# Expert 0's weights split by ACT and DVE in the gap between two stages, in place of POOL during attention

## What is computed

```python
x = x + attention(layernorm(x), ctx, ctx)     # 16 heads of 16, rope, window of 64 keys
x = x + experts(layernorm(x))

def experts(x):                               # E = 8 experts, hidden size 1024
    probs = softmax(x @ router_w.T)
    p, i = top_k(probs, 2); p = p / p.sum(-1)
    for e in range(8):
        mask = (i == e).any(-1)
        mean_w = (p * (i == e)).sum() / max(mask.sum(), 1)
        h = silu(x @ gate_w[e].T) * (x @ up_w[e].T)
        out += mask * (h @ down_w[e].T) * mean_w
```

## Time and profile before

| | |
|---|---|
| median of 3 runs | 505.71 us (504.89 to 505.95) |
| the profiled execution | 505.44 us, its span from first to last instruction 503.5 us |
| PE busy | 447.7 us (89%) |
| DVE busy | 308.0 us (61%) |
| ACT busy | 264.9 us (53%) |
| POOL busy | 139.0 us (28%) |
| the chain of work that ended last | PE 65%, DVE 14%, issue 6%, ACT 6%, POOL 4%, DMA 3% |
| mean granted clock of TensorE | 0.96 |

### The profile page before, as it was taken

How to read it: one execution, slowest core, us unless ns; L and a number is a source line. 1 busy time by engine, 2 the same in 40 slices (tenths; PEclk the granted TensorE clock), 3 DMA queues, 4 the chain that set the end, 5 groups by cost and what they waited for, 6 DMA issues and landing times.

```text
span 503.5 us, 8805 instructions
## 1 busy us (share of the span) xinstructions
PE 447.7 (89%) x2747; PEld 365.6 (73%) x2747; DVE 308.0 (61%) x721; ACT 264.9 (53%) x847; POOL 139.0 (28%) x130
## 2 busy tenths in 40 slices
PE   3999999898988999517999999999999999999980
PEld 2656565565655565316999999999999999999980
DVE  3566889898989867542754737646366463663320
ACT  1297867676766778203545545546365453544330
POOL 5201135262717163340005023040130401304013
PEclk9999999999999999755999999999999999999996
DMA  7075202020202025435464546645465453312003
GB/s 231 28 208 196 79 21 64 5 63 6 62 7 61 8 59 176 152 92 149 126 199 77 168 127 152 191 83 160 136 143 178 87 161 114 38 38 33 6 0 36
DMA packets 23597, 49.36 MB, mean 98 GB/s; under 512 B 5288, under 2 KB 15080, under 8 KB 23292
## 3 DMA queue, kind: packets, MB, share of 16 engines
q10 hardware_dynamic: 6302, 23.29, 15.1%
q1 hardware_dynamic: 11102, 18.51, 11.9%
q0 software_dynamic: 6144, 6.97, 8.4%
HBM read 38.51 MB, written 12.74 MB: 102 GB/s over the span
## 4 chain that ended last, share of the span: by engine, by line
PE 65%; DVE 14%; issue 6%; ACT 6%; POOL 4%; DMA 3%; ACTq 1%; DVEq 0%; SPq 0%; POOLq 0%
PE b_o L638 9%; PE b_small L638 9%; PE b_s L625 8%; PE b_s L626 8%; PE b_s L627 8%; PE b_s L424 3%; ACT probs L743 3%; PE b_pt L625 3%; PE b_pt L627 3%; PE b_pt L626 3%; DVE negmax L994 2%; PE b_proj L478 2%; DVE xn L860 2%; PE b_pv L447 2%; DMA rows_sb<-in_rownum 2%
## 5 line engine op out<-in xcount | busy, mean ns | idle before, releaser
L743 ACT ACTIVATE probs<-b_s,negmax 100x100 f32<-100x100 f32 x256 | 85.6, 360 | 33.2 <-DVE negmax L994 33.0
L1192 POOL DMA_INDIRECT out<-y_sb,idnow x32 | 48.7, 1523 | 181.5 <-ACT y_sb L789 174.2
L772 ACT CAST h_hi<-h_sb 128x448 fp32r<-128x448 f32 x64 | 36.3, 567 | 88.1 <-DVE h_sb L1080 88.1
L625 PE MATMUL b_s<-x_hi,w_hi 128*128 128x448 f32 x192 | 72.4, 377 | 0.7 <-DVE x_lo L1070 0.7
L626 PE MATMUL b_s<-x_lo,w_hi 128*128 128x448 f32 x192 | 71.6, 373 | 0.0
L627 PE MATMUL b_s<-x_hi,w_lo 128*128 128x448 f32 x192 | 71.5, 372 | 0.0
L1084 DVE TENSOR_TENSOR h_lo<-h_sb,h_hi 128x448 fp32r<-128x448 f32 x64 | 40.2, 628 | 40.5 <-ACT h_hi L772 40.5
L1089 DVE TENSOR_TENSOR w_lo<-w_raw,w_hi 128x1024 fp32r<-128x1024 f32 x42 | 51.5, 1225 | 13.6 <-ACT w_hi L777 13.6
L743 ACT ACTIVATION_READ_ACCUMULATOR probs<-b_s,negmax 100x1 f32 x256 | 56.7, 221 | 0.0
L424 PE MATMUL b_s<-kblk,qrot 128*100 128x400 f32 x128 | 54.3, 506 | 0.0
L1080 DVE TENSOR_TENSOR h_sb<-b_s,act 128x448 f32<-128x448 f32 x32 | 19.8, 620 | 45.1 <-PE b_s L627 45.1
(11 more groups left out here) (133 smaller groups left out, 964.2 us busy)
## 6 DMA issues: line engine op xcount, KB each, us to landing
w_raw<-in_ffw ACTq DMA_DIRECT2D x36, 512.0 KB, 3.9
xin<-slots SPq DMA_DIRECT2D x9, 449.8 KB, 4.5
slots<-in_padrows SPq DMA_DIRECT2D x8, 449.8 KB, 4.6
w_raw<-in_ffw ACTq DMA_DIRECT2D x1, 3072.0 KB, 10.1
w_raw<-in_ffw SPq DMA_DIRECT2D x6, 512.0 KB, 6.6
kblk<-krot SPq DMA_DIRECT2D x128, 12.5 KB, 1.8
out<-x_all SPq DMA_DIRECT2D x8, 200.0 KB
ctx_all<-in_ctxT SPq DMA_DIRECT2D x1, 1200.0 KB, 6.1
```

The lines of the kernel that those rows point to most:

```text
L625: pe.matmul(o, wh[:, c, cols], x_hi[:, c, :], start=(c == 0), stop=False)
L743: m = nc.scalar.activation(probs[:, N % 3, h, :], b_s[N % 3][0:S, h * S:(h + 1) * S], ACT.Exp, bias=negmax[:, N % 4, h:h + 1], accum_out=p ...
L772: nc.scalar.copy(h_hi[:, f, :], h_sb[:, f % 2, :]).then_inc(s_hhi, 1)
L1192: G.indirect_dma_start(out, bass.IndirectOffsetOnAxis(idnow[:, n:n + 1], 0), y_sb[:, n, :], None, bounds_check=TOK + TILE - 1, oob_is_err= ...
```

## The change

POOL no longer splits expert 0's weights. ACT issues their load in pair 1 as six chunks in place of one. After the last exponentials of attention, at `n == 0` of `i == 9`, ACT casts all six chunks, ahead of its copy `xn2T` of the last pair. DVE subtracts two chunks at the same place of its list, ahead of the last pair's `logits`, and the other four after `meanw`, ahead of the experts. SP no longer loads expert 1's weights; ACT issues these six loads after it has cast `x_hi` of the first tile, each when its chunk of `w_raw` has been subtracted. The counts that later waits look for are moved by one load accordingly.

```diff
@@ sync
-            sp.wait_ge(s_wlo, WCH)
-            for k in range(WCH):
-                sp.dma_start(w_raw[:, k * WC:(k + 1) * WC], ffw[1][:, k * WC:(k + 1) * WC]).then_inc(s_raw[k], 16)
             store_x2(NPAIR - 1)
@@ scalar
+            def weights_high(e, par, k):
+                a.wait_ge(s_raw[k], 16 * (e + 2))
+                cols = slice(k * WC, (k + 1) * WC)
+                nc.scalar.copy(w_hi[1 - par][:, cols], w_raw[:, cols]).then_inc(s_whi, 1)
+
                         nc.scalar.copy(probsT[:, M % 3].rearrange("p h s -> p (h s)"),
                                        b_pt[0:S, 0:QH * S]).then_inc(s_pTc, 1)
+                    if n == 0 and i == NPAIR + 1:
+                        for k in range(WCH):
+                            weights_high(-1, 1, k)
                     if n == 0 and 0 <= i - 2 < NPAIR:
                         x2_copy(i - 2)
                     if n == 1 and i == 1:
-                        a.dma_start(w_raw[:, :], ffw[0]).then_inc(s_raw0, 16)
+                        for k in range(WCH):
+                            a.dma_start(w_raw[:, k * WC:(k + 1) * WC],
+                                        ffw[0][:, k * WC:(k + 1) * WC]).then_inc(s_raw[k], 16)
...
             x_high(0)
+            for k in range(WCH):
+                reload(-1, k)
             for e in range(E - 1):
                 expert(e, e % 2, e + 2 < E)
@@ vector
+            def weights_low(e, par, k):
+                v.wait_ge(s_whi, WCH * (e + 1) + k + 1)
+                cols = slice(k * WC, (k + 1) * WC)
+                V.tensor_tensor(w_lo[1 - par][:, cols], w_raw[:, cols], w_hi[1 - par][:, cols],
+                                ALU.subtract).then_inc(s_wlo, 1)
...
+                    if n == 0 and i == NPAIR + 1:
+                        for k in range(2):
+                            weights_low(-1, 1, k)
                     if n == 2 and 0 <= i - 2 < NPAIR:
                         choose(i - 2)
...
             V.tensor_tensor(meanw[:, :], b_o[:, 0:E], crec[:, :], ALU.mult).then_inc(s_mean, 1)
+            for k in range(2, WCH):
+                weights_low(-1, 1, k)
             v.wait_ge(s_first, 1)
@@ gpsimd
-                if 1 <= i < 7:
-
-                    g.wait_ge(s_raw0, 16)
-                    cols = slice((i - 1) * WC, i * WC)
-                    G.tensor_copy(w_hi[0][:, cols], w_raw[:, cols]).then_inc(pool_self, 1)
-                    ps[0] += 1
-                    g.wait_ge(pool_self, ps[0])
-                    G.tensor_tensor(w_lo[0][:, cols], w_raw[:, cols], w_hi[0][:, cols],
-                                    ALU.subtract).then_inc(s_wlo, 1)
```

## The result

The changed kernel takes 499.53 us in the median (498.88 to 499.83), the kernel before beside it 505.72 us; the ratio is 0.9879, with a 95% interval of 0.9862 to 0.9896. The profiled execution took 498.88 us, its span 496.9 us. The forecast was 497.0 us, with a range of 493.0 to 502.0 us. The direction and the mechanism were right; the gain of pair 2 and the price of the six issues in pair 1 were mis-sized.

The account below looks back on a forecast made before the run. Attention was taken as the stage that matters, with DVE's xn stalled beside POOL's split in five pairs. Terms -9.7 + 0.8 + 0.2 = -8.7 us gave 497.0 us from a 505.71 us median, range 493.0 to 502.0 us.

Parts of the forecast that it names:

- The stall and what it gives back: Attention: DVE's xn no longer waits for POOL's split; L510 comes 1.94 us earlier, pair pitch falls from 24.38 to 22.44 us.
- DVE's 2.80 us: Start of a pair: xn ready 3.54 - 0.74 = 2.80 us earlier, the upper end of what a pair can give back.
- PE's 3.18 us: Undisturbed pair 1: PE's time from the start of the key projection to L510, put onto the later pairs.
- less comes back: Rival, attention: PE sheds only its 1.17 us wait per pair; 3.9 us faster in all, 501.8 us; chance 0.15.
- more comes back: Rival, attention: the whole 2.80 us of a pair returns, issues absorbed; 14.0 us gained, 491.7 us; chance 0.12.
- Five times 1.94: Attention, pairs 2 to 6: five meetings of xn with POOL's split give back 1.94 us each, 9.7 us in all.
- The six issues in pair 1: Pair 1: five more issues at 0.334 us hold ACT 1.67 us, making L510 late; cost 0.8 us, bounds 0 and 1.67.
- The gap's work: Gap: ACT's six casts and DVE's six subtractions are hidden; only the last scatter's issue is stretched, costing 0.2 us.
- one far over 1.4 us in all: Sign of being wrong: a scatter beside a subtraction taking far over 1.4 us.
- The port in the gap: Rival, gap: POOL's last scatter cannot write descriptors while DVE subtracts; 4.5 us later, 501.5 us; chance 0.06.
- The moved load: Expert stage: ACT's six issues of expert 1's weights take 2.0 us; first Silu 0.95 us late, all hidden.
- slower: Rival, expert stage: expert 1's weights come too late and PE starves; 510.8 us if landing takes 20 us; chance 0.03.
- no relief: Rival, attention: xn stays long for a reason other than POOL's split; 505.7 to 506.7 us; chance 0.03.

Follow-up runs that it names:

- the half split: Changed kernel, but POOL again casts and subtracts 512 columns of a chunk at its old place in pairs 1 to 6: 501.73 us, ratio 0.9908.
- The run with spread issues: Changed kernel, but the six loads of pair 1 are issued one with each of the steps n = 1 to 6: 497.33 us, ratio 0.9816.
- the best kernel that moved it to two other engines: Changed kernel with one load issue in pair 1 and all six DVE subtractions behind the mean weights: 495.78 us; on another chip 496.88 us.

## Why the prediction was right or wrong

*The stall and what it gives back* was right. The forecast pitch was 22.44 us; measured were 22.48, 22.48 and 22.41 us. The step that carried it was not to take DVE's 2.80 us but to ask what is late next, and to read PE's 3.18 us from an undisturbed pair. The rivals "less comes back" and "more comes back" fall with this, and the half split shows how the cost of the stall grows.

*Five times 1.94* was a little high: the five gave 9.14 us in place of 9.7. Pair 2 gave 1.48 us. There PE starts its key projection 2.12 us after `rstd` (63.98 against 61.86 us in the kernel before), and 1.64 us after it in pair 3 (87.88 against 86.24 us). The stall had covered the difference; without it, it counts. I had read one pair and multiplied.

*The six issues in pair 1* are the term that was mis-sized: 0.8 us forecast, bounds 0 and 1.67 us, and the profiles show 2.0 us (23.77, 23.38, 23.01 and 23.54 us for pair 1 with the six, 20.99 to 21.98 us in six profiles with one), and 1.7 us more in the three profiles where TensorE's clock fell behind the wait (24.69 to 25.24 us), which no term had. The mechanism was the one named, PE waiting at L506 for ACT's `xnT`. The price was wrong, because the row has issues that stand 3 us apart; in a row each takes half as much again. The run with spread issues confirms 0.334 us alone. This one term put the forecast 1.2 to 2 us too low. The right price stood in the trace of the kernel before, in SP's timeline, where six issues of the same loads follow each other:

```profile
194.27 3.28 SPq L364 DMA_DIRECT2D w_raw<-in_ffw  x6
```

At that price ACT is held 2.95 us longer than by one issue, `xnT` ends at 48.37 us, and L510 is 2.06 us late.

*The gap's work* was right: six casts and six subtractions are hidden. The 0.2 us is luck in part. It was forecast as a stretch of the last scatter, which was not stretched at all; 0.2 us came by a way that I had set aside, the early subtractions, which hold a scatter that then holds DVE's `choice`. I had forecast a stretch of up to 0.35 us and named one far over 1.4 us in all as a sign of being wrong; it was 1.5 us, 2.46 us in all. *The port in the gap* was therefore nearer than its 0.06: the block exists. It missed the path because the last scatter starts 0.45 us ahead of the subtractions.

*The moved load* was right in that nobody waits for the weights. That it is hidden was right only in part: these six issues took 2.94 us in place of 2.0, DVE's product came to wait for the Silu, and where TensorE's clock rose early PE waited too, 0.2 to 0.6 us in three profiles of this placing. The rivals "slower" and "no relief" fall.

Together: -9.1 + 2.0 + 0.2 gives -6.9 us, and the medians show -6.2 and -6.7 us. The falls of the clock in pair 1 can make up the difference; no run shows how often they come.

## What to carry to other kernels

When DVE and POOL each have an instruction on SBUF at the same time, look at the durations of both before asking which engine should do the work: moving POOL's part by one place in its list gave as much as the best kernel that moved it to two other engines, and 3 us more than the change as it was made. Price a stall by replaying the next engine's sequence from an undisturbed round, for each round and not once. Price transfers at the place where they are issued: six issues in a row cost 3 us of ACT where one costs 0.33 us, and 3 MB on one queue lengthened both transfers on the critical path of another by 1.7 to 3.8 us. And read the granted clock behind a new wait of PE before putting a loss down to the edit next to it.

## What the runs showed of the hardware

- A scatter's issue on POOL that begins while DVE runs a subtraction of two SBUF operands is held to its end: it began at 206.07 us, DVE was done at 207.67 us, and it ended at 208.53 us, 2.46 us against 0.99 us. One that had begun before the subtraction was not stretched (0.98 us at 216.29 us), and didn't hold it either: the four subtractions behind it took 4.62 us, no more than four single ones of the experts' stage (1.23 us each). The Trainium skill (SBUF — State Buffer, section Who interferes with whom) has the rule that the second to come is blocked, and infers that descriptor writing is spared beside a two-operand instruction. The trace agrees with the rule where the scatter came second, so a scatter's issue as a whole isn't spared; where it came first, neither held the other. Which part of the issue waits no run shows.
- Issues of 512 KB loads on ACT took 0.334 us each when 2 to 4 us apart, and 2.85 to 3.06 us for six in a row in pair 1; on SP six in a row took 3.28 us.
- After the gap, with TensorE idle but for a few transposes, its products ran at half the granted clock (1.2 GHz) for 3.0 to 6.1 us before it rose to 2.4 GHz, in kernels and executions that do the same ahead of it. That is up to 1.4 us from one execution to the next (a product every 0.37 us in place of 0.205 us), as much as some of the effects looked for here.
- In attention, behind waits of PE of 1.75 to 1.97 us in pair 1, the granted clock stayed at 2.4 GHz in four profiles and fell to 1.2 GHz for some 3.3 us in three, which cost 1.7 us each.
